# Moving the split of the second pair's gated outputs in one block of a two-layer Mamba-2 and channel-mix kernel

## What is computed

```python
zxbcdt = u @ in_w.T                        # 512 -> z 1024, x 1024, B and C 128, dt 16
z, xBC, dt = jnp.split(zxbcdt, [D_INNER, D_INNER + CONV_DIM], axis=-1)
dt = jax.nn.softplus(dt + dt_bias)
xBC = jax.nn.silu(causal_conv4(xBC) + conv_b)       # four taps, each channel by itself
# scan over time, for each of 16 heads:
state = dA_t * state + (dt_t * x_t) * B_t
y_t = state @ C_t
y = ys + Dp * xh
y = y * jax.nn.silu(z)                               # the gate
y = y * jax.lax.rsqrt(jnp.mean(y * y, -1, keepdims=True) + EPS) * rms_w
return y @ out_w.T
```

## Time and profile before

| What | us |
|---|---|
| median of three runs | 4825.02 |
| the profiled execution by itself | 4828.47 |
| span of its trace | 4826.7 |
| TensorE matmul busy | 4096.1 |
| VectorE busy | 3357.0 |
| ScalarE busy | 2922.8 |
| GpSimd busy | 2002.1 |

### The profile page before, as it was taken

How to read it: one execution, slowest core, us unless ns; L and a number is a source line. 1 busy time by engine, 2 the same in 40 slices (tenths; PEclk the granted TensorE clock), 3 DMA queues, 4 the chain that set the end, 5 groups by cost and what they waited for, 6 DMA issues and landing times. The chain is left out here.

```text
span 4826.7 us, 100096 instructions
## 1 busy us (share of the span) xinstructions
PE 4096.1 (85%) x38872; PEld 3622.3 (75%) x38872; DVE 3357.0 (70%) x5217; ACT 2922.8 (61%) x4904; POOL 2002.1 (41%) x1572
## 2 busy tenths in 40 slices
PE   4399888888889899956989898989898998499999
PEld 1388888888878788846878888888888888377777
DVE  7377777777777777745777777777777777466664
ACT  4466666666666666635666666666666666466664
POOL 7134333333333334421333343434343444466664
PEclk6699999999999999978999999999999999699999
DMA  8300000000000000020000000000000000322220
GB/s 310 105 27 28 28 28 28 28 28 28 28 28 28 28 28 28 23 73 26 28 28 27 28 27 28 27 28 27 28 27 28 27 29 28 110 83 88 83 87 36
DMA packets 108673, 220.99 MB, mean 46 GB/s; under 512 B 10760, under 2 KB 11272, under 8 KB 107272
## 3 DMA queue, kind: packets, MB, share of 16 engines
q1 hardware_dynamic: 108176, 214.25, 12.6%
HBM read 146.97 MB, written 67.24 MB: 44 GB/s over the span
## 5 line engine op out<-in xcount | busy, mean ns | idle before, releaser
L501 PE MATMUL l_ring<-l_u_hi,l_wi_lo 128*128 128x256 f32 x4608 | 1312.9, 285 | 81.0 <-ACT l_raw L742 72.4
L501 PE MATMUL l_ring<-l_u_lo,l_wi_hi 128*128 128x256 f32 x4608 | 1298.1, 282 | 0.0
L501 PE MATMUL l_ring<-l_u_hi,l_wi_hi 128*128 128x256 f32 x4608 | 1296.9, 281 | 0.0
L974 DVE SCALAR_TENSOR_TENSOR l_xc<-l_raw,l_prm,l_xc 128x256 f32<-128x256 f32 x1536 | 852.3, 596 | 232.6 <-ACT l_xc L751 214.4
L501 PEld LDWEIGHTS l_ring<-l_u_hi,l_wi_lo 128*128 128x128 f32 x4608 | 876.4, 190 | 105.7 <-ACT l_raw L742 85.9
L501 PEld LDWEIGHTS l_ring<-l_u_lo,l_wi_hi 128*128 128x128 f32 x4608 | 876.1, 190 | 8.9
L501 PEld LDWEIGHTS l_ring<-l_u_hi,l_wi_hi 128*128 128x128 f32 x4608 | 874.6, 190 | 0.0
L1149 POOL TENSOR_TENSOR l_g<-l_g 128x512 f32<-128x512 f32 (+2 forms) x384 | 347.0, 904 | 926.8 <-ACT l_g L812 906.7
L1120 POOL TENSOR_TENSOR l_rhs<-l_cum,l_small 32x1024 fp32r<-32x1024 f32 x256 | 496.3, 1939 | 514.8 <-PE l_wide L563 474.1
L1006 DVE TENSOR_TENSOR l_e<-l_e,l_ps_m 128x1024 f32<-128x1024 f32 x256 | 312.8, 1222 | 414.2 <-ACT l_e L800 410.2
L501 PE MATMUL l_ring<-l_wo_hi,l_g_lo 128*128 128x512 f32 x1024 | 411.9, 402 | 82.9 <-DVE l_g_lo L1026 82.9
(11 more groups left out here) (162 smaller groups left out, 8335.2 us busy)
## 6 DMA issues: line engine op xcount, KB each, us to landing
l_hn<-h_scratch SPq DMA_DIRECT2D x64, 512.0 KB, 4.0
l_res<-h_scratch SPq DMA_DIRECT2D x128, 256.0 KB, 3.8
h_scratch<-l_res SPq DMA_DIRECT2D x128, 256.0 KB, 2.1
m_rows<-in_x SPq DMA_DIRECT2D x16, 1024.0 KB, 9.5
h_scratch<-m_rows SPq DMA_DIRECT2D x16, 1024.0 KB, 7.7
f_x<-in_x SPq DMA_DIRECT2D x16, 1024.0 KB, 6.1
f_h<-h_scratch SPq DMA_DIRECT2D x16, 1024.0 KB, 8.2
out<-f_x SPq DMA_DIRECT2D x64, 256.0 KB, 2.0
```

The lines of the kernel that those rows point to most:

```text
L501: last = nc.tensor.matmul(out, a, c, start=(k == 0), stop=(k == n - 1))
L974: ins = nc.vector.scalar_tensor_tensor(out=acc, in0=raw[:, k, tap:tap + TB], scalar=prm_sb[:, w:w + 1], in1=acc, op0=ALU.mult, op1=ALU.add)
```

## The change

On ScalarE the order after `new_state(1, 1)` was `conv_in(3)`, `silu_x(2)`, `z_read(3)`, `high_g(1)`, `conv_in(4)`; it becomes `silu_x(2)`, `high_g(1)`, `conv_in(3)`, `z_read(3)`, `conv_in(4)`. On VectorE `low_g(1)` moves from behind `taps(3)` to between `taps(2)` and `taps(3)`. No instruction is added or removed. GpSimd, TensorE and the DMA queues issue what they did, in the order they did.

```diff
@@ -839,10 +839,11 @@
                     silu_x(*nxt, 1)
                 new_state(b, s, 1, 1)
                 if n1:
+                    silu_x(*nxt, 2)
+                high_g(b, s, 1)
+                if n1:
                     conv_in(*nxt, 3)
-                    silu_x(*nxt, 2)
                     z_read(*nxt, 3)
-                high_g(b, s, 1)
                 if n1:
                     conv_in(*nxt, 4)
                 if n2:
@@ -1074,9 +1075,9 @@
                 finish(b, s, 0)
                 if n1:
                     taps(*nxt, 2)
+                low_g(b, s, 1)
+                if n1:
                     taps(*nxt, 3)
-                low_g(b, s, 1)
-                if n1:
                     taps(*nxt, 4)
                 if n2:
                     split_u(*nxt2)
```

More of the change, by code:

```diff
@@ L1076, in body @@
                     taps(*nxt, 2)
-                    taps(*nxt, 3)
                 low_g(b, s, 1)
                 if n1:
+                    taps(*nxt, 3)
                     taps(*nxt, 4)
```

## The result

The changed kernel takes 4981.1 us (median of 4 runs, 4979.2 to 4988.6), against 4825.9 for before on the same chip: a ratio of 1.0325 (95% interval 1.0307 to 1.0343), 155 us slower. The prediction was 4955 with a range of 4905 to 4995, so the time lies inside the range, 26 us above the forecast.

A forecast was written before the change was run, and what follows sets the result against it. A chain through several engines, without slack from taps 2 to the next pass, was taken as the bound. 60 passes x (1.49 us order + 0.7 us clock), less 1, gave 130 us and a median of 4955, range 4905 to 4995.

The forecast's parts named there:

- What bounds the kernel: From the end of taps 2 to the next pass, a chain through several engines has no slack; no engine's sum bounds it.
- Term 1: Ahead of the read of projection 6, `silu_x(2)` and `high_g(1)` add 0.52 + 0.97 = 1.49 us a pass; bounds 1.4 and 1.68.
- What is taken out pays nothing back: Behind that read on ScalarE, and for `low_g(1)` on VectorE, the moved work was hidden, so its removal gains nothing.
- TensorE's stalls: Ahead of projection 8 from 1.15 to 2.64 us, for `g_lo` gone, ahead of the square sum from 0.62 to about 1.9.
- Term 2: TensorE's clock falls around projection 8 after the 2.64 us stall, costing the chain 0.7 us in every pass.
- A pass has one or the other, as the first fall fills the second stall: A clock fall at projection 8 rules out another at the stall ahead of the square sum, priced up to 3.0 us.
- The two passes without `nxt2`: The output product's 1.99 us stall set the end of these passes and goes, a gain of about 0.4 us each.
- Sum: 60 x (1.49 + 0.7) = 131, less 1, is 130 us over the passes, giving a median of 4955.
- (a): TensorE's clock holds, so only the 1.49 us of order counts in 60 passes: 88 us, 4913; chance 0.20.
- (b): TensorE sets the pass, so only the output product's 0.25 us later end counts: 15 us, 4840; chance 0.04.
- (c): Faster: TensorE's projection 6 or 7 gates the read, not the taps; 69 us less, 4756; chance 0.04.
- (d): Both stalls bring clock falls, or the second costs its upper price in 4 passes of 10: 185 us, 5010; chance 0.11.

The follow-up runs named there:

- ScalarE's part: Only ScalarE's reorder (`silu_x(2)` and `high_g(1)` ahead of `conv_in(3)`) against the kernel before, `low_g(1)` left behind taps 3; 4970.3 us, ratio 1.0299.

## Why the prediction came out as it did

- **What bounds the kernel:** right. The kernel with `high_g` moved and nothing else in the chain stayed at 4828, silu alone added its own time, and with the clock held the whole change costs what stands in the chain.
- **Term 1, the order:** right in mechanism, 1.33 us for the 1.49 predicted and below the lower bound of 1.4. Within the stretch from silu to read the sum fits (1.48). The 0.15 is at its head, where I had set the start after taps 2 equal for the read and for silu, which starts sooner behind its releaser.
- **"What is taken out pays nothing back":** right. The wait for `g_lo` went, VectorE waited 0.68 us for the first taps with `low_g` done, and nothing came of it.
- **TensorE's stalls:** predicted 2.64, none and 1.9; measured 2.48, none and 1.95.
- **Term 2, the clock:** right that the clock would fall and that this was worth about half; wrong in place and size, and this is the step that failed: "I take 0.7 in every pass, as the 2.64 us stall comes first and is the longer". The fall came behind the second, shorter stall, at the head of the next pass, where the chain runs through TensorE's front and projection 0 (the fences at the end of this section). It cost 1.44 us. The bounds of 0 to 3.0 held it. Where the fall did come at projection 8, in the kernel of ScalarE's part, the price was 60.72 - 59.96 = 0.76 us, so the 0.7 was the right price for the wrong place. "A pass has one or the other, as the first fall fills the second stall" was wrong too: a fall at projection 8 brought the second stall down to 1.2 or 1.3 us, and the clock fell behind it all the same.
- **The two passes without `nxt2`:** a gain of 0.4 us each was predicted; the passes went from 55.9 to 59.5, and with both stalls filled still to 57.3. So the order is in their chain as well. The product's stall had not set their end: in the filled kernel with `high_g` ahead and `low_g` early that stall is gone, and they take 55.9 as before. With `low_g` early it is the pass behind them that becomes shorter: in the first layer the two passes together, with what lies up to the second layer, went from 207.2 to 208.3 us, and with both stalls filled to 206.1.
- **Sum:** two errors partly cancel, and that the forecast came within 26 us is in part luck. The 47 inner passes were predicted to lose 47 x 2.19 = 103 us and lost 133; the 11 at a return were counted as the others, 24 us, and lost 11. Eight of these take 65.0 to 65.2 us and three, which have half clock at projection 8 as well, 67.4 to 67.7; with both stalls filled all eleven take 65.5 to 65.9. Their average is then the same 65.7, so the falls that the change adds there and those that it spares come out even.
- **Rivals:** (a), that the clock holds, did not happen, but its price was right: the kernel with both stalls filled, where the clock does hold, takes 4905 for 4913. (b) and (c) fell with it. (d), both stalls, happens in 8 of 47 inner passes of ScalarE's part (62.2 us); in the changed kernel half clock at both places occurs in eight passes in all, of which one is an inner pass. The Trainium skill (TensorE: Matmul & The Clock Gate, "Why this matters for your kernels") warns only of idle gaps longer than any stall in an inner pass of the changed kernel. The clock fell behind stalls of 2.0 and 2.5 us, so here the measurement decides against it.
- **What would show it:** the silu behind taps 2, the read behind it, the missing wait for `g_lo` and the stall ahead of projection 8 came as described. PEclk of 8 in the slices did not: they are steady 9s, as before. Line 501's products are slow in few passes; it is the front that runs at half clock.

ScalarE's wait for projection 0 behind the seam, from its timeline, before and in the changed kernel:

```profile
1555.89 0.48 ACT L716 ACTIVATE l_dtx<-l_ring,l_prm 128x256 f32<-128x256 f32 x1 [0.40 <-PE l_ring L501]
...
1609.95 0.48 ACT L716 ACTIVATE l_dtx<-l_ring,l_prm 128x256 f32<-128x256 f32 x1 [1.85 <-PE l_ring L501]
```

And the same wait over the whole trace (total, times, longest), of before:

```profile
ACT l_dtx L716 <- PE l_ring L501: 68.7, 64, 6.3
```

of the changed kernel:

```profile
ACT l_dtx L716 <- PE l_ring L501: 136.1, 64, 6.3
```

and of the changed kernel with both stalls filled, where the line is 724:

```profile
ACT l_dtx L724 <- PE l_ring L501: 62.4, 64, 6.3
```

At the seam shown the wait grew by 1.85 - 0.40 = 1.45 us, which is the whole 1.44. Over the trace it grew by 67 us, and with the clock held and the order kept it is back at 62.4: it is there that the half clock reaches the chain.

What stays open: why, in the changed kernel, the fall comes behind the 1.95 us stall in nearly every pass and behind the 2.48 us stall in few, while both kinds of pass occur in the kernel of ScalarE's part. What TensorE does right behind the stall differs (small products and transposes behind the one, dense products behind the other), and so does the moment at which the stall comes; the runs don't separate the two.

## What to carry to other kernels

An instruction that waits for an event holds back everything behind it in its queue: work that could run in the idle time ahead of the event must stand ahead of the waiting instruction. `high_g` was free there (4828 us) and cost 0.95 us a pass behind the waiting silu. A stall on an engine that is not the bound is still not free on TensorE, where two microseconds may be paid for again at half clock; what a fall costs depends on whether the work behind it is in the chain. When such a stall can't be removed, a few products into a free PSUM tile can be cheaper than none.

## What the runs showed of the hardware

- With one program and stalls of 1.99 and 2.00 us at the same place, the clock fell in one pass and not in another. The third passes of the last sequences, with `high_g` alone moved, are a second case: behind a stall of 1.98 us each, the output product ran at a clock of 0.77 in the first layer and of 1.00 in the second. Windows from the product's start:

```profile
2077.80:2085.20 7.40, 7.40 (x27) 5.90 (x27) 4.23 (x6) 4.49 (x6) 2.88 (x3) 0.77 0.00 0
4089.30:4096.70 7.40, 7.40 (x40) 6.22 (x40) 4.98 (x8) 4.48 (x6) 3.44 (x4) 1.00 0.00 0
```

- With stalls of at most 1.5 us in the inner passes (silu alone ahead) the clock fell in none of them. Where projection 8 had run at half clock until some 10 us before, it fell again behind 1.1 to 1.3 us (ScalarE's part alone). Behind the 3.3 us and more at the loop's return it fell always.
- What a fall costs depends on its place: 0.76 us at projection 8, 1.44 to 1.6 us at the head of a pass.
- A TensorE with more work was faster: seven added products of 512 columns in a pass took 55 us off 4875 (1.2%), sixteen took 76 us off 4981 (1.5%).
- VectorE's six tap instructions take 2.71 us alone and 3.74 us with GpSimd's sums beside them; `split_u` takes 0.68 alone and 1.78 with them. Moving the sums moved the cost from one to the other.
